# A fourth score tile transposed beside TensorE, weight loads issued by ACT, and no loop

## The reference, cut to what is computed

```
h = layernorm(x) * (1 + ca) + sa                    # ca, sa, ga, ... from silu(c) @ wmod
q, k, v = h @ Wq + bq (scaled), h @ Wk + bk, h @ Wv + bv      # 16 heads of 128
q, k = rotary(q), rotary(k)                         # t*cos + rotate_half(t)*sin
attn = softmax(causal(q @ k.T)) @ v
x = x + ga * (attn @ Wo + bo)
h = layernorm(x) * (1 + cb) + sb
x = x + gb * down(silu(gate(h)) * up(h))            # weights as integers with scales
```

## Time and profile before

| | |
|---|---|
| Median of 3 runs | 970.95 us (970.11 to 971.28) |
| The profiled execution's own time | 968.9 us |
| Its span, first to last instruction | 967.0 us |
| Granted TensorE clock, mean | 0.995 of full speed |
| PE busy | 934.2 us (97%) |
| POOL busy | 774.9 us (80%) |
| DVE busy | 735.9 us (76%) |
| ACT busy | 673.4 us (70%) |
| DMA, mean | 146 GB/s, 141.63 MB |

### The profile page before, as it was taken

How to read it: one execution, slowest core, us unless ns; L and a number is a source line. 1 busy time by engine, 2 the same in 40 slices (tenths; PEclk the granted TensorE clock), 3 DMA queues, 4 the chain that set the end, 5 groups by cost and what they waited for, 6 DMA issues and landing times.

```text
span 967.0 us, 20178 instructions
## 1 busy us (share of the span) xinstructions
PE 934.2 (97%) x5667; PEld 833.6 (86%) x5667; DVE 735.9 (76%) x1582; ACT 673.4 (70%) x1354; POOL 774.9 (80%) x555
## 2 busy tenths in 40 slices
PE   6989999999999999999999999999999999878898
PEld 5878998888889989989998888889989989767787
DVE  6766877778878877787877877887878777867544
ACT  5766766677677767676767677777777676757763
POOL 2468988898898988898889888998889888795653
PEclk9999999999999999999999999999999999999999
DMA  7554554554445545554455554644555545531011
GB/s 256 163 137 137 179 166 142 159 182 154 140 136 175 167 136 158 179 167 150 145 156 174 169 150 133 183 148 139 156 170 168 158 147 171 177 95 44 1 44 46
DMA packets 108978, 141.63 MB, mean 146 GB/s; under 512 B 12948, under 2 KB 80084, under 8 KB 108884
## 3 DMA queue, kind: packets, MB, share of 16 engines
q1 hardware_dynamic: 108884, 140.72, 48.5%
HBM read 62.36 MB, written 44.76 MB: 111 GB/s over the span
## 4 chain that ended last, share of the span: by engine, by line
PE 87%; DVE 3%; POOL 3%; issue 2%; ACT 2%; DMA 1%; SPq 0%; POOLq 0%; DVEq 0%; ACTq 0%
PE ps_r L1565 18%; PE ps_r L1564 18%; PE ps_r L1563 18%; PE ps_s L1563 7%; PE ps_s L1565 7%; PE ps_s L1564 7%; PE ps_t L1728 5%; PE ps_s L1570 1%; PE ps_s L1573 1%; PE ps_r L1570 1%; PE ps_r L1572 1%; PE ps_r L1668 1%; ACT probs L1046 1%; POOL pT_lo L782 1%; DMA wmod_a<-in_L_wmod 1%
## 5 line engine op out<-in xcount | busy, mean ns | idle before, releaser
L1046 ACT ACTIVATE probs<-ps_s,neg_max 128x128 f32<-128x128 f32 (+7 forms) x256 | 189.8, 742 | 84.5 <-DVE neg_max L1451 82.3
L764 POOL TENSOR_TENSOR swapped<-swapped,sin_sb 128x512 f32<-128x512 f32 x124 | 161.2, 1300 | 94.4 <-DMA swapped<-straight 94.1
L1451 DVE CUSTOM_DVE_ANT_0 ps_s<-ps_s,mask_wide 128x128 f32<-128x128 f32 (+7 forms) x256 | 193.6, 756 | 14.8 <-PE ps_s L1565 12.4
L782 POOL TENSOR_TENSOR pT_lo<-side_p,pT_hi 128x1024 fp32r<-128x1024 f32 (+2 forms) x93 | 195.3, 2131 | 0.7 <-ACT pT_hi L1035 0.7
L773 POOL TENSOR_TENSOR qk_lo<-swapped,qk_hi 128x512 fp32r<-128x512 f32 x124 | 159.4, 1297 | 19.7 <-ACT qk_hi L930 19.6
L767 POOL TENSOR_TENSOR swapped<-swapped,qk_cos 128x512 f32<-128x512 f32 x124 | 161.3, 1301 | 10.5
L1563 PE MATMUL ps_s<-qk_hi 128*128 128x512 f32 (+4 forms) x384 | 142.1, 370 | 2.4 <-ACT probs L1046 2.3
L1379 DVE STREAM_TRANSPOSE squares<-probs 128x1024 f32<-128x1024 f32 (+2 forms) x93 | 103.1, 1109 | 51.6 <-ACT probs L1046 48.4
L1565 PE MATMUL ps_r<-pT_hi,v_lo 128*128 128x512 f32 (+3 forms) x384 | 133.0, 346 | 0.0
L1564 PE MATMUL ps_r<-pT_lo,v_hi 128*128 128x512 f32 (+3 forms) x384 | 132.6, 345 | 0.0
L1565 PE MATMUL ps_s<-qk_hi,qk_lo 128*128 128x512 f32 (+4 forms) x384 | 131.4, 342 | 0.0
(11 more groups left out here) (205 smaller groups left out, 2409.3 us busy)
## 6 DMA issues: line engine op xcount, KB each, us to landing
swapped<-straight SPq DMA_DIRECT2D x252, 128.0 KB, 2.7
side_out<-squares SPq DMA_DIRECT2D x31, 512.0 KB, 2.6
side_p<-side_out SPq DMA_DIRECT2D x124, 128.0 KB, 2.9
side_out<-squares SPq DMA_DIRECT2D x31, 448.0 KB, 2.6
side_p<-side_out SPq DMA_DIRECT2D x124, 112.0 KB, 2.6
side_out<-squares SPq DMA_DIRECT2D x31, 384.0 KB, 2.3
side_p<-side_out SPq DMA_DIRECT2D x124, 96.0 KB, 2.2
x_in<-in_L_attn_x SPq DMA_DIRECT2D x4, 512.0 KB, 5.6
```

The costliest lines, as they stand in the source:

```text
L764: pool.tensor_tensor(swapped[:, q, :], swapped[:, q, :], sin_sb[:, at_], ALU.mult).then_inc(rotated, 1)
L782: pool.tensor_tensor(turned_at(t, 0, t + 1)(pT_lo).rearrange("p k (i c) -> p k i c", c=SQUARE), from_squares(side_p[t], t)[:, t::-1, :, :] ...
L1046: nc.scalar.activation(halved(t, probs[:, P_AT[step] * P:(P_AT[step] + t + 1) * P]), score_rows(step, t), ACT.Exp, bias=neg_max[:, t:t + 1 ...
L1451: nc.vector.tensor_tensor_reduce(rows, rows, halved(t, mask_wide[:, SEQ - n_keys:SEQ]), -1.0, -MASKED, ALU.add, ALU.min, accum_out=neg_max ...
```

## The change

- `SIDE` takes in tile 4. PE no longer transposes it: `turn:7.0-` and `turn:7.1-` go from the plans of PE, ACT and DVE (in the last unit, which has no side tiles, they stay in `ENDING`). DVE gets `side:7-` (squares) and `lower:7-` (the low part, by `side_lower`), SP `side:7-` and `back:7-`, ACT `side:7-`. `side_p` of tile 4 lies where that of tile 7 lies, so each one's read back waits until the other's low part is made.
- All five plans are written in a new order; `raw:` moves from SP's plan to ACT's (`load_raw`), among its conversions.
- The loop is gone: each engine's units 1 to 31 are written out.
- In `PLANS_30` and `PLANS_31` the order is new too: in unit 31 `scores:3` and `make:W00-` come ahead of `make:P1-`, `sum:W00-` ahead of `turn:1.0`, `moments:0` after `max:5`, `float:1` after `exp:4`.

The core of the diff, with one line of each kind of plan:

```
-SIDE = (7, 6, 5)
+SIDE = (7, 6, 5, 4)
...
-SYNC_PLAN = """swap:K0+ swap:Q0+ | side:1 back:1 side:3 swap:K1+ swap:Q1+ back:3 side:5 back:5 raw:K raw:Q raw:V raw:O"""
+SYNC_PLAN = """side:7- swap:K0+ swap:Q0+ back:7- | side:1 back:1 swap:K1+ side:3 swap:Q1+ back:3 side:5 back:5"""
...
-                    elif what == "raw":
-                        if x == WO:
-                            sp.wait_ge(w_ready[WV], ps.passes(piece + 1))
-                        else:
-                            sp.wait_ge(w_ready[WO if x == WV else x], ps.passes(piece))
-                        load_w(x, ps.passes(piece))
...
-            with sp.Fori(0, LAST) as i:
-                run(Span(1, 1 + UNITS, i))
-            run(Span(ALL_UNITS - 3, ALL_UNITS + 1))
+            run(Span(1, ALL_UNITS + 1))
...
+            def load_raw(ps, j, n):
+
+                if j == WO:
+                    act.wait_ge(w_ready[WV], ps.passes(n + 1))
+                    src = wo_t[:, bass.ds(ps.passes(n) * 2, 2), :]
+                else:
+                    act.wait_ge(w_ready[WO if j == WV else j], ps.passes(n))
+                    src = w_t[j][:, :, bass.ds(ps.passes(n) * 2 * DH, 2 * DH)]
+                act.dma_start(w_buffers[j][0], src).then_inc(raw_ready[j], 16)
...
-            with pe.Fori(0, LAST) as i:
-                run(Span(1, 1 + UNITS, i))
-            run(Span(1 + LAST * UNITS, ALL_UNITS))
+            run(Span(1, ALL_UNITS))
```

More of the change, by code:

```diff
@@ L130 @@
 PLANS_29 = {
-    SYNC_PLAN: """swap:K0+ swap:Q0+ | side:1 back:1 side:3 swap:K1+ swap:Q1+ back:3 load:0 side:5 back:5 load:1"""}
+    SYNC_PLAN: """side:7- swap:K0+ swap:Q0+ back:7- | side:1 back:1 swap:K1+ side:3 swap:Q1+ back:3 load:0 side:5 back:5
+        load:1"""}
 PLANS_30 = {
-    TENSOR_PLAN: """scores:0 turn:6.0- make:K0+ make:Q0+ turn:7.0- scores:1 make:P0- scores:2 turn:7.1- make:K1+ make:Q1+
-        turn:0.0 scores:3 make:W00- scores:4 make:P1- turn:2.0 scores:5 make:W01- make:L0 make:W10- make:L1
-        turn:4.0 scores:6 make:L2 make:W11- make:L3 scores:7 make:L4 make:L5""",
@@ L138 @@
[L138 to L142 removed]
+    TENSOR_PLAN: """make:K0+ turn:6.0- scores:0 make:Q0+ scores:1 make:P0- scores:2 make:K1+ make:Q1+ turn:0.0 scores:3
+        make:W00- turn:2.0 scores:4 make:P1- make:W01- scores:5 make:W10- make:L0 scores:6 make:W11- make:L1
+        turn:4.0 scores:7 make:L2 make:L3 make:L4 make:L5""",
@@ new lines @@
+    SCALAR_PLAN: """exp:7- out:K0+ turn:6.0- out:Q0+ exp:0 side:5- high:P0- exp:1 out:K1+ exp:2 out:Q1+ side:7- high:K0+
+        turn:0.0 turn:2.0 exp:3 high:Q0+ float:0 exp:4 float:1 high:P1- side:1 float:2 exp:5 out:L0 high:K1+
+        out:L1 exp:6 turn:4.0 out:L2 side:3 out:L3 high:Q1+ out:L4 out:L5""",
+    VECTOR_PLAN: """side:7- max:0 cos:K0+ turn:6.0- cos:Q0+ max:1 low:P0- max:2 side:1 cos:K1+ cos:Q1+ lower:7- max:3
+        sum:W00- turn:0.0 max:4 side:3 turn:2.0 largest:0 low:P1- sum:W01- max:5 sum:W10- max:6 sum:W11- side:5
@@ L143 @@
         largest:1 max:7 turn:4.0""",
[L144 removed]
+    SYNC_PLAN: """side:7- swap:K0+ swap:Q0+ back:7- load:2 side:1 back:1 swap:K1+ side:3 swap:Q1+ back:3 side:5 back:5
+        load:3"""}
 PLANS_31 = {
[L148 to L150 removed]
@@ L151 @@
-    SCALAR_PLAN: """out:K0+ exp:7- turn:6.0- exp:0 out:Q0+ side:5- turn:7.0- turn:7.1- float:3 high:P0- turn:0.0 exp:1 exp:2
-        high:P1- exp:3 turn:1.0 turn:1.1 turn:2.0 exp:4 gated:0 out:D0 turn:3.0 exp:5 turn:3.1 turn:4.0 out:D1
-        exp:6 turn:5.0 out:D2 turn:5.1""",
-    VECTOR_PLAN: """max:0 turn:6.0- turn:7.0- largest:2 turn:7.1- max:1 low:P0- max:2 turn:0.0 largest:3 low:P1- max:3
-        turn:1.0 sum:W00- turn:1.1 max:4 moments:0 turn:2.0 sum:W01- width:X max:5 turn:3.0 sum:W10- turn:3.1
-        turn:4.0 sum:W11- max:6 max:7 turn:5.0 turn:5.1""",
@@ L157 @@
-    SYNC_PLAN: """load:4 load:5"""}
+    TENSOR_PLAN: """make:K0+ make:Q0+ scores:0 turn:6.0- scores:1 make:P0- scores:2 turn:0.0 scores:3 make:W00- make:P1-
+        turn:1.0 scores:4 turn:1.1 turn:2.0 make:W01- make:X scores:5 make:D0 turn:3.0 make:W10- turn:3.1
+        turn:4.0 make:W11- scores:6 make:D1 turn:5.0 scores:7 make:D2 turn:5.1""",
+    SCALAR_PLAN: """out:K0+ exp:7- turn:6.0- exp:0 out:Q0+ side:5- high:P0- exp:1 turn:0.0 exp:2 side:7- exp:3 float:3
+        high:P1- turn:1.0 turn:1.1 turn:2.0 exp:4 gated:0 out:D0 turn:3.0 exp:5 turn:3.1 turn:4.0 out:D1 exp:6
+        turn:5.0 out:D2 turn:5.1""",
@@ L160 @@
+    VECTOR_PLAN: """side:7- max:0 turn:6.0- max:1 low:P0- max:2 turn:0.0 max:3 lower:7- sum:W00- largest:2 low:P1- largest:3
+        turn:1.0 turn:1.1 max:4 turn:2.0 sum:W01- width:X max:5 moments:0 turn:3.0 sum:W10- turn:3.1 turn:4.0
+        sum:W11- max:6 max:7 turn:5.0 turn:5.1""",
+    SYNC_PLAN: """side:7- back:7- load:4 load:5"""}
 ENDING = {
```

44 lines of the change are left out of this document (15 added, 29 removed).

## The result

The changed kernel takes **977.39 us** (median of 6 runs, 974.1 to 980.55), the kernel before 970.65 in the same comparison (970.11 to 971.31): ratio 1.007, 95% interval 1.0055 to 1.0086. It is slower by 6.7 us, where 959.7 and faster was forecast. The profiled execution took 976.3 us, with a span of 974.3, 7.3 more than before. The runs also lie further apart: 6.4 us instead of 1.2.

What follows compares the result with a forecast made beforehand. PE's own work was taken to bound the kernel. -15.4 (transpositions) + 4.2 (P1's wait) = -11.2 us, other terms at nothing: 957.7 profiled, 959.7 us as median forecast, range 952.5 to 971.

Steps and rivals of the forecast that it cites:

- The bound: 28 units from 100 to 825 us: PE never idles, so its own work is the 25.90 us period.
- The transpositions, 0.55 us a unit: Tile 4's transpositions leave PE: 0.44 + 0.11 us per unit, 15.4 us saved over 28 units.
- P1's wait, 0.15 us a unit: P1 waits for lower:7-, delayed by POOL beyond 0.13 us of slack: 4.2 us lost, bounds 0 and 1.17 per unit.
- The average phase (0.53): Mean delay behind P1 if POOL's phase against lower:7- were arbitrary: 0.53 us, result 970.4.
- The two inputs in SBUF: lower:7- on DVE waits for the POOL operation under way, costing it 0 to 1.30 us.
- ACT's issues, 0: 28 weight-load issues move from SP to ACT: 0 on the path, at most 3 us.
- POOL and the swaps, 0: Swaps queue behind back:1, which waits for lower:7-; POOL idles 2.5 us per unit without harming PE, so no cost.
- No loop, 0: Removing the seven branches brings nothing back; fetch stalls up to 2 us as the other bound.
- the rival's fall: Rival: fetching without the loop stalls PE or DVE at ends of blocks, 970 to 985; chance 0.06.
- The first units, 0 to 1.7 gained: Three units outside the saturated stretch (0, 1's beginning, 30) also lose transpositions: counted 0, at most 1.7 us.
- The last two units, 0 (-2 to +2): Reordered end: PE's waits could shrink, but P1 of unit 30 awaits tile 4 through memory; taken as 0.
- The rival that ended on the other side: lower:7- waits for POOL in every unit, P1's delay exceeds the saving: 970.4 average phase, 988 worst; chance 0.13.

Runs made afterwards that it cites:

- run 9: Kernel before, with each of tile 4's five transpositions on PE made twice in all units but the last: 986.3 us, ratio 1.0167.
- run 2: Changed kernel with the subtraction lower:7- replaced from unit 1 on by an in-place transposition with one SBUF input: 968.98 us, ratio 0.997.
- run 13: Changed kernel with one added wait: POOL begins the rotation of Q0+ only when lower:7- on DVE is done: 994.69 us, ratio 1.0251.
- run 10: Changed kernel with ACT's conversions of Q1 and V1 ahead of side:3 and POOL's split:K one rotation earlier: 984.66 us, ratio 1.0159.
- run 17: Changed kernel with SP's write side:3 ahead of swap:K1+ in all units, as in the kernel before: 998.74 us, ratio 1.0282.
- run 5: Changed kernel with the raw weights loaded by SP again, behind tile 5's reads: 984.72 us, ratio 1.0134.
- run 1: Kernel before with its seven rounds of four units written out, no loop, nothing else: 971.62 us, ratio 1.0006.
- run 4: Changed kernel with SP's write side:3 ahead of swap:K1+ again in unit 1 alone: 976.0 us, ratio 1.0053.
- run 18: The kernel of run 15 with P0's low parts last as well: 963.94 us, ratio 0.9924.
- run 14: Changed kernel with tile 4 of units 29 and 30 on PE again and the old plans of units 30 and 31: 975.44 us, ratio 1.0049.
- run 3: Changed kernel with P1's 8 low-part matmuls placed last, behind the wait for lower:7-: 973.6 us, ratio 1.0027.
- run 15: Changed kernel, P1's low parts last, Q1/V1 conversions ahead of side:3, split:K earlier, side:3 ahead of swap:K1+ in unit 1, old end: 967.57 us, ratio 0.9966.

## Why the prediction was wrong, point by point

- **The bound.** Right: PE's own work is the unit of the kernel before, and only of that one.
- **The transpositions, 0.55 us a unit.** Right: 0.54 by run 9, 15 us in 28 units.
- **P1's wait, 0.15 us a unit.** This is the step that failed most. The mechanism was named and is shown (runs 2 and 13), and the place too; the size was taken from a walk through the order with POOL in one phase, "nearer the walk than the average". Measured: 0.29 on PE's step and 0.06 behind it, 0.35 in all; 28 x 0.20 = 5.6 us more than the sum has. The slack of 0.13 was near (0.09), and POOL lengthened `lower:7-` in 23 of 28 units. The average phase (0.53) would have been as far off on the other side: its 970.4 is nearer to 977.39 only because other terms were at nothing. The phase is not a given of the order either: `lower:7-` lasts 1.18 us on average in the changed kernel, 1.41 in run 10, 1.45 in run 17, by small moves elsewhere.
- **Other places of PE with no slack.** Not in the prediction at all, a term at nothing without a reason: 0.06 at V0 and 0.12 at V1, 5 us in 28 units, because in the new order PE reaches their banks as DVE frees them. A unit without P1's wait therefore is 25.53 and not 25.35. The account of a unit: 25.90 - 0.55 + 0.18 + 0.35 = 25.88, against 25.90 measured.
- **The two inputs in SBUF.** The direction was right: by the Trainium skill, SBUF — State Buffer, section Who interferes with whom, a DVE instruction with two SBUF inputs contends with a GpSimd instruction that reads SBUF. The trace agrees, with 0.81 us becoming up to 1.95.
- **ACT's issues, 0.** Right in the loop (run 5 is slower with the loads on SP); at the head 2.8 us go with them (run 5's head), by a wait and the clock behind it.
- **POOL and the swaps, 0, "POOL idles 2.5 us per unit with no harm to PE".** Wrong as a reason, though the changed order itself is not late: 1.3 us less of that idle time cost 17 us in run 13, and the other order of SP cost 21 in run 17.
- **No loop, 0.** Right (run 1), and so is the rival's fall. The Trainium skill's rule on taken branches (Runtime: NRT & Kernel Launch, Instruction fetch mechanics) gives no time here: 971.62 without a branch, 971.05 with seven.
- **The first units, 0 to 1.7 gained.** Wrong: 4.5 us lost. Runs 4 and 5 find 2.8 of them in tile 6's way through memory with the weight loads beside it, some 1.7 of these by the clock that fell behind the wait. Of the other 1.7, 1.2 lie between 72.3 and 85.4 us, where PE waits 0.81 for `lower:7-` (0.30 for POOL at the same P1 before); with P1's low parts last 0.6 of them are left (run 18: 12.50 us, before 11.89).
- **The last two units, 0 (-2 to +2).** 2.9 us lost, all of it undone in run 14's profile. How much is the new order and how much the clock (0.57 in one window) stays open.

In the profiled execution the forecast was -11.2 and +7.3 came: 18.5 apart. 11.1 of it is in the 28 units (-11.2 forecast, -0.1 measured), 4.5 the head, 2.9 the end.

The rival that ended on the other side had the cause and was given 0.13. It decided "from a delay of 0.55 us behind P1"; in fact 0.35 were enough, since 0.18 went elsewhere. Nor did it take a meeting in every unit, or more loss behind P1 than the change saves: in the profile the units alone came out even, and the loss is in the two ends.

## What to carry to other kernels

When work is taken from an engine that is full, ask of every other place where it waits how much slack is left, not only of the wait that the change adds; here three places without any idle time before (P1, V0, V1) took back all of 0.55. A wait that can't be made shorter can be moved down: the part of a product that doesn't need the late operand goes first (runs 3, 15, 18), at no cost that they show, and then even an operation that lasts twice as long is harmless. And idle time of an engine in a ring (POOL, SP's queue, DMA, ACT, back to POOL) is not slack: test it with one added wait before counting on it. Where the clock can fall, look at the granted clock of the windows behind each long wait too: in the head it cost nearly as much as the wait.
